# Moving the mapped product of attention one step earlier in a pipelined transformer block

## The chip, the cores and the metric

The kernel runs on one core of a Trainium2 chip. The metric is the device time of one execution in microseconds, the median of several. The core has TensorE (PE, matmuls), VectorE (DVE), ScalarE (ACT), GpSimd (POOL) and SyncE (SP, which here issues all DMAs). Each works through a program of its own; they meet only at semaphores. Matmul results land in PSUM, a memory of eight banks.

## The reference

One pre-normalised transformer block on x of 32 sequences, 256 tokens, 128 channels, in fp32:

```
x = x + attention(layernorm(x))        # 16 heads of 8, causal local window of 64
x = x + ffn(layernorm(x))

attention: q, k, v = x Wq', x Wk', x Wv'; query i sees key j with i-64 < j <= i
           softmax(q k' / sqrt(8)) v, then Wo
ffn:       scores = sigmoid(x gate_kernel) + bias, 16 experts in 4 groups
           the 2 best groups by the sum of their top 2, in them the 4 best experts
           weights normalised to sum 1, times 2.5
           y = sum over experts of weight * (silu(x w_gate) * (x w_up)) w_down
           + silu(x sw_gate) * (x sw_up) sw_down      # shared expert, width 128
```

## The kernel before

The work is cut into 16 groups (NG) of 2 sequences, 512 tokens each. One group passes through a chain of numbered stages (the constants `XT`, `QP`, `SC`, `PV`, `OT`, ... at the top), from 3 to 36. A slot has 8 steps (`STEPS`), and a stage n is done in step n % 8 of slot g + n // 8: five groups are under way at any time, so each step holds attention scores of one group, the expert work of an older one, and bits of others. Slots 0 to 3 and 16 to 19 are written out, slots 4 to 15 are a loop over pairs of slots. Each engine's block has a function `slot` that runs over the steps 0 to 7 and, within a step, over its pieces in a fixed order, written out by hand. That order and the semaphores are all that sets the time: an engine that waits holds everything behind it.

In each step there are, for one of eight units: gate and up projection on TensorE (L895 to L897, three matmuls each), tanh and a copy of the gate on ScalarE (`th` L597, `gate`), `tu` on VectorE (L798), two products on GpSimd (`gate2` L504, `hh` L509) and the down projection (L1077) one step later; and for one of eight attention units: a mask and scores on TensorE (L921, L933), row maxima on VectorE (`neg_max` L809), exponentials on ScalarE (`probs` L626), and a step later the transposition (`probsT` L765) and sums of the probabilities (`sums` L775).

Around the change, for each of the two halves b of a group (one sequence each):

- `turn_sums(b)` on VectorE (L783, L784): the reciprocals of the softmax sums, and their transposition. Stage `TURN[b]`.
- the spread on GpSimd (L482): each reciprocal is laid out by block of 32 queries, `by_block`. Stage `EXPAND[b]`. It waits for the transposition (`s_sum_t`).
- the spreading matmul on TensorE (L1037) with `to_channel`, which maps the reciprocals to channels, into a shared PSUM bank; then the mapped product on VectorE, `oT = o_f * bank` (L833), which is the last reader of that bank. Stage `OT + 4b`.
- the output projection (L1047) and the residual `H` (L840), stage `OW + 4b`; statistics for the second normalisation and, on GpSimd, the normalisation itself (L542 to L553, stages `LN2`, `LN2 + 4`), its transposition on TensorE (L1063, `XT2`), copied by ScalarE (`x_f`, `x_hi`).

Two PSUM banks are shared by many short uses (`RING`, `USES`): the attention inputs (`XT`, `QP`, `KP`, `VP`), the routing logits (`LG`, L963), the combine weights (`CT`, L1086), the shared expert (`SH`), `OT`, `OW`, `XT2`. The list is sorted by step and, within a step, by place (EARLY, POST, LATE, WEIGHTS), and the uses take the two banks in turn. TensorE, before it fills a bank (`free`), waits until the last use of that same bank has been taken by its reader. So the routing logits at the start of step 0 wait for whoever used their bank last, and so do the transposes of the combine weights in step 3, whatever data they need.

Of the kernel before, what the change touches and what calls it, by code (L numbers as in the profile page):

```python
# [49 lines left out]
SUMS = (11, 12, 13, 13, 14, 14, 15, 16)  # L50
TURN = (14, 16)
EXPAND = (15, 17)
OT, OW = 15, 16
LN2 = 17
# [16 lines left out]
    (EARLY, (VP, LG)), (LATE, (XT, QP, KP, XT2, XT2 + 4, SH)),  # L71
    (POST, (OT, OT + 4, OW, OW + 4, SH)), (WEIGHTS, (CT,)))
    for stage in stages])
# [11 lines left out]
def at(slot, s, stage, stride=1, count=1):  # L85

    for k in range(count):
        d = stage + k * stride
        if d % STEPS == s:
            off = d // STEPS  # L90
            if slot.fixed and not 0 <= slot.n - off < NG:
                return None, 0
            return Group(slot.n - off, (slot.par + off) % 2, slot.fixed), k
    return None, 0

# [87 lines left out]
def preln_block_kernel(nc, x, w_att, gate_b, w_gu, w_down, sw_down, consts, out):  # L183
    with ExitStack() as ctx:
# [269 lines left out]
        def _(pool):  # L454
# [8 lines left out]
            def slot(sl):  # L463
                for s in range(STEPS):
                    if sl.fixed and sl.n == 1 and s == PREPARE:
# [8 lines left out]
                           ALU.subtract).then_inc(s_cst, 1)  # L474
                    for b, stage in enumerate(EXPAND):
                        g, _ = at(sl, s, stage)
                        if g:
                            if not (g.fixed and g.n == 0):
                                taken(pool, slot_before(sl), (OT + 4 * b) % STEPS, POST)
                            pool.wait_ge(s_sum_t, g.n * GB + b + 1)  # L480
                            whole = [P, NQ, Q]
                            tt(by_block[:, b, :, :], sums_t[:, b, :].unsqueeze(1).broadcast_to(whole),  # L482
                               block_of[:, :].unsqueeze(2).broadcast_to(whole), ALU.mult).then_inc(s_exp, 1)
                    if sl.fixed and sl.n == 0 and s == LN1 + 1:
# [45 lines left out]
                    if g and part == 1:  # L530
# [4 lines left out]
                           sc3.rearrange("p n (g e) -> p n g e", e=4),  # L535
                           g_in[:, :, :].unsqueeze(3).broadcast_to([P, NT, N_GROUP, 4]), ALU.mult).then_inc(s_rp, 1)
                    g, b = at(sl, s, LN2, 4, GB)
                    if g:
# [130 lines left out]
        def _(dve):  # L669
# [72 lines left out]
            def slot(sl):  # L742
# [3 lines left out]
                for s in range(STEPS):  # L746
# [80 lines left out]

                    g, b = at(sl, s, OT, 4, GB)
                    if g:
# [32 lines left out]
                    if g and draining(sl):  # L862
                        dve.wait_ge(s_g2, g.n * NP + k + 1)
                        dve.wait_ge(s_tu, g.n * NP + k + 1)
                        v_.tensor_tensor(hh[:, k % 2, :], gate2[:, :], tu[:, k % 2, :], ALU.mult).then_inc(s_h, 1)  # L865
                    turn_sums(0)
                    sum_probs()
                    turn_sums(1)
                    g, _ = at(sl, s, YE)
# [20 lines left out]
        def _(pe):  # L890
# [48 lines left out]
            def slot(sl):  # L939
                for s in range(STEPS):  # L940
# [69 lines left out]
                    for turn_, stage in enumerate(PV):  # L1010
# [6 lines left out]
                        if not later and not (g.fixed and g.n == 0 and b == 0):  # L1017
                            taken(pe, slot_before(sl) if b else sl, (OT if b else OT + 4) % STEPS, POST)
                        pe.wait_ge(s_pt, g.n * NU + 4 * b + (4 if later else 3))
# [10 lines left out]

                    g, b = at(sl, s, OT, 4, GB)
                    if g:
# [7 lines left out]
                    if g:  # L1040
                        side, bank = free(POST)
                        taken(pe, sl if b else slot_before(sl), (OT + 4 * b) % STEPS, POST)
                        if g.fixed and g.n == 0 and b == 0:
                            pe.wait_ge(s_wf, 16 * FFN_LOADS)
                        for half in range(2):
                            r = slice(P * half, P * half + P)
                            ins = mm(bank[:, r], oT[:, r], wo[:, :], start=True, stop=True)  # L1047
                        ins.then_inc(s_filled[side], 1)
# [96 lines left out]
```

## Time and profile before

| | |
|---|---|
| median of 3 runs | 715.27 us (715.05 to 715.5) |
| profiled execution | 716.24 us, its span 714.4 us |
| TensorE busy | 659.0 us, 92% |
| VectorE busy | 588.1 us, 82% |
| ScalarE busy | 525.8 us, 74% |
| GpSimd busy | 495.6 us, 69% |
| mean granted clock of TensorE | 0.994 |

The span is the time between the first and the last instruction that the profile shows; the execution's own time has a little around it. Busy shares are sums of instructions' durations. A matmul's row ends after the next one has begun, so TensorE's rows overlap, and their sum isn't quite time in which nothing else could have run. In the timeline rows the bracket at the end gives the idle time of the engine ahead of the row, and who ended it.

### The profile page before, as it was taken

What the parts mean: (1) busy time and instruction counts of PE and PEld (TensorE: products, weight loads), DVE (VectorE), ACT (ScalarE), POOL (GpSimd) and SP (SyncE); (2) the same over time, 40 slices, a digit from 0 to 9 for tenths busy, and PEclk for the clock granted to TensorE, in tenths of its full rate; (3) what the DMA queues carried; (4) which work ended last, traced back from release to release, by engine and by line L of the source; (5) the groups of instructions that cost most, each with busy time, mean ns of one, the idle gap of its engine ahead of it and who ended that gap; (6) DMA issues with size and microseconds to landing.
All of it is one profiled execution on the core that took longest, in us unless ns stands there. A gap on an engine that the chain in (4) does not pass through costs nothing.

```text
span 714.4 us, 19501 instructions
## 1 busy us (share of the span) xinstructions
PE 659.0 (92%) x6232; PEld 521.2 (73%) x6232; DVE 588.1 (82%) x1710; ACT 525.8 (74%) x1603; POOL 495.6 (69%) x635
## 2 busy tenths in 40 slices
PE   3989889999999999999999999999999999989997
PEld 2877767777777777777777777777777777777875
DVE  3687888888889897889889897988979888897663
ACT  3786778697878878787887878787887878764332
POOL 4413367778778787878778777777878777876523
PEclk9999999999999999999999999999999999999999
DMA  5010032230403132140413123040322214040321
GB/s 173 1 32 30 2 101 66 59 123 11 141 29 119 59 105 73 40 138 2 142 34 119 59 76 102 2 147 29 119 59 96 82 32 119 15 135 33 118 77 45
DMA packets 50245, 52.60 MB, mean 74 GB/s; under 512 B 5664, under 2 KB 31904, under 8 KB 50080
## 3 DMA queue, kind: packets, MB, share of 16 engines
q1 hardware_dynamic: 50208, 52.14, 23.6%
q8 instruction: 20, 0.33, 0.2%
q14 instruction: 17, 0.14, 0.1%
HBM read 43.20 MB, written 4.72 MB: 67 GB/s over the span
## 4 chain that ended last, share of the span: by engine, by line
PE 42%; DVE 24%; ACT 19%; issue 10%; POOL 2%; DVEq 1%; DMA 1%; ACTq 0%; POOLq 0%; SPq 0%
ACT probs L626 9%; PE PS L1077 6%; PE PS L933 6%; DVE neg_max L809 6%; PE PS L895 5%; PE PS L1024 5%; PE PS L897 5%; PE PS L896 5%; ACT q_by_head L581 5%; DVE tu L798 4%; DVE probsT L765 3%; PE PS L1047 3%; DVE sums L775 3%; PE PS L963 2%; ACT k_by_row L581 2%
## 5 line engine op out<-in xcount | busy, mean ns | idle before, releaser
L626 ACT ACTIVATE probs<-PS,neg_max 128x96 f32<-128x96 f32 (+1 forms) x1024 | 246.8, 350 | 87.7 <-DVE neg_max L809 87.5
L504 POOL TENSOR_TENSOR gate<-gate,spread 128x512 f32<-128x512 f32 x124 | 158.1, 1275 | 96.6 <-ACT gate L581 40.8
L509 POOL TENSOR_TENSOR hh<-gate,tu 128x512 f32<-128x512 f32 x108 | 138.7, 1284 | 19.3 <-DVE tu L798 12.8
L809 DVE TENSOR_REDUCE neg_max<-PS 128x4 f32<-128x384 f32 (+1 forms) x256 | 121.6, 513 | 25.5 <-PE PS L933 25.0
L1077 PE MATMUL PS<-wd,hh 128*128 128x128 f32 x1024 | 137.9, 278 | 3.5 <-DVE hh L865 1.7
L1077 PEld LDWEIGHTS PS<-wd,hh 128*128 128x128 f32 x1024 | 126.5, 192 | 12.2 <-issue 4.3
L798 DVE SCALAR_TENSOR_TENSOR tu<-th,PS 128x512 f32<-128x512 f32 x128 | 87.4, 683 | 48.5 <-ACT th L597 36.6
L895 PE MATMUL PS<-x_hi,w_hi 128*128 128x512 f32 x288 | 125.0, 434 | 0.0
L897 PE MATMUL PS<-x_lo,w_hi 128*128 128x512 f32 x288 | 114.7, 398 | 0.0
L765 DVE STREAM_TRANSPOSE probsT<-probs 128x768 f32<-128x768 f32 (+1 forms) x128 | 114.4, 894 | 0.0
L896 PE MATMUL PS<-x_hi,w_lo 128*128 128x512 f32 x288 | 114.0, 396 | 0.0
L597 ACT ACTIVATE th<-PS 128x512 f32<-128x512 f32 x128 | 79.5, 621 | 42.6 <-PE PS L897 39.5
L933 PE MATMUL PS<-k_by_row,q_by_head 64*128 64x192 f32 (+2 forms) x1024 | 108.3, 318 | 0.0
L775 DVE TENSOR_REDUCE sums<-probs 128x8 f32<-128x768 f32 (+1 forms) x128 | 106.3, 851 | 0.0
L933 PEld LDWEIGHTS PS<-k_by_row,q_by_head 64*128 64x128 f32 x1024 | 84.6, 191 | 0.0
L581 ACT ACTIVATE gate<-PS 128x512 f32<-128x512 f32 x128 | 79.6, 622 | 0.0
L897 PEld LDWEIGHTS PS<-x_lo,w_hi 128*128 128x128 f32 x288 | 54.4, 189 | 12.7
L895 PEld LDWEIGHTS PS<-x_hi,w_hi 128*128 128x128 f32 x288 | 54.7, 190 | 10.8 <-issue 3.1
L896 PEld LDWEIGHTS PS<-x_hi,w_lo 128*128 128x128 f32 x288 | 54.7, 190 | 7.3
L921 PEld LDWEIGHTS PS<-band,ident 64*128 64x128 bf16 x320 | 14.4, 93 | 59.3 <-issue 30.2
L1024 PE MATMUL PS<-probsT,v_bd 128*32 128x96 f32 (+2 forms) x2048 | 51.1, 241 | 0.0
L921 PE MATMUL PS<-band,ident 64*128 64x256 bf16 (+2 forms) x320 | 38.8, 253 | 12.7 <-ACT probs L626 12.1
(107 smaller groups left out, 991.3 us busy)
## 6 DMA issues: line engine op xcount, KB each, us to landing
spread<-weights_by_expert SPq DMA_DIRECT2D x248, 128.0 KB, 3.0
X<-x SPq DMA_DIRECT2D x32, 256.0 KB, 3.6
OUT<-H SPq DMA_DIRECT2D x16, 256.0 KB, 3.0
out<-OUT SPq DMA_DIRECT2D x16, 256.0 KB, 3.8
ffn_stage<-w_gu SPq DMA_DIRECT2D x1, 1152.0 KB, 6.7
wd<-w_down SPq DMA_DIRECT2D x1, 512.0 KB, 6.8
weights_by_expert<-cT SPq DMA_DIRECT2D x16, 32.0 KB, 1.6
probsT<-w_att SPq DMA_DIRECT2D x1, 192.0 KB, 3.1
```

The source lines that it names most:

```text
L504: tt(gate2[:, :], gate[:, k % 2, :], spread[:, k % SP_BUFS, :], ALU.mult).then_inc(s_g2, 1)
L509: tt(hh[:, k % 2, :], gate2[:, :], tu[:, k % 2, :], ALU.mult).then_inc(s_h, 1)
L581: return nc.scalar.activation(dst, src, ACT.Copy, **kw)
L626: ins = nc.scalar.activation(probs[:, u % PROB_BUFS, tt, 2 * rows + e, j0:KW], PS[:, rows, n * KW + j0:n * KW + KW], ACT.Exp, bias=neg_max ...
L765: v_.transpose(probsT[:, b, :, t0:t0 + 2, c0:3, :].rearrange("p g t c q -> p t g (c q)"), probs[:, u % PROB_BUFS, :, :, c0 * Q:KW]).then_i ...
L775: v_.tensor_reduce(sums[:, b, HG * t0:HG * t0 + 2 * HG], probs[:, u % PROB_BUFS, :, :, j0:KW].rearrange("p t g k -> p (t g) k"), AX_X, ALU ...
L809: v_.tensor_reduce(neg_max[:, rows, :], src[:, :, j0:KW], AX_X, ALU.max, negate=True).then_inc(s_m, 1)
L895: mm(dst, l_hi, r_hi, start=True, stop=False)
L896: mm(dst, l_lo, r_hi, start=False, stop=False)
L897: return mm(dst, l_hi, r_lo, start=False, stop=True)
L933: ins = mm(dst[:, :, KW - nk:KW], q_by_head[r, g.par, q1 // Q - 1, :, :].rearrange("p v q -> p (v q)"), k_by_row[r, g.par, :, q1 - nk:q1], ...
L1077: ins = mm(PS[:, 7, r], hh[:, k % 2, r], wd[:, k, :], start=(k == 0 and n == 0), stop=(k == NP - 1), skip_group_check=True)
```

## The change

Nothing is computed in another way, and each engine has the same instructions. What differs is the steps:

- the reciprocals of the first half are turned at stage 13 instead of 14: in step 5, after the sums, instead of step 6, ahead of them (those of the second half stay at stage 16, step 0);
- the spread on GpSimd goes to the same stages as the turning (13 and 16), and its code stands after the routing pieces and ahead of the second normalisation, not at the start of a step;
- the spreading matmul and the mapped product go from stages 15 and 19 (steps 7 and 3) to 14 and 18 (steps 6 and 2). The shared banks are dealt out anew by the same rule.

```diff
-TURN = (14, 16)
-EXPAND = (15, 17)
-OT, OW = 15, 16
+TURN = (13, 16)
+EXPAND = (13, 16)
+OT, OW = (14, 18), 16
...
-    (POST, (OT, OT + 4, OW, OW + 4, SH)), (WEIGHTS, (CT,)))
+    (POST, (*OT, OW, OW + 4, SH)), (WEIGHTS, (CT,)))
...
+def either(slot, s, stages):
+
+    for b, stage in enumerate(stages):
+        g, _ = at(slot, s, stage)
+        if g:
+            return g, b
+    return None, 0
...
@@ GpSimd: gone from the start of a step, ahead of the products of the experts
-                    for b, stage in enumerate(EXPAND):
-                        g, _ = at(sl, s, stage)
-                        if g:
-                            if not (g.fixed and g.n == 0):
-                                taken(pool, slot_before(sl), (OT + 4 * b) % STEPS, POST)
-                            pool.wait_ge(s_sum_t, g.n * GB + b + 1)
...
@@ GpSimd: now behind the routing, ahead of LN2
+                    for b, stage in enumerate(EXPAND):
+                        g, _ = at(sl, s, stage)
+                        if g:
+                            if not (g.fixed and g.n == 0):
+                                taken(pool, slot_before(sl), OT[b] % STEPS, POST)
+                            pool.wait_ge(s_sum_t, g.n * GB + b + 1)
+                            whole = [P, NQ, Q]
+                            tt(by_block[:, b, :, :], sums_t[:, b, :].unsqueeze(1).broadcast_to(whole),
+                               block_of[:, :].unsqueeze(2).broadcast_to(whole), ALU.mult).then_inc(s_exp, 1)
                     g, b = at(sl, s, LN2, 4, GB)
...
@@ VectorE
-                    g, b = at(sl, s, OT, 4, GB)
+                    g, b = either(sl, s, OT)
...
-                    turn_sums(0)
                     sum_probs()
-                    turn_sums(1)
+                    for b in range(GB):
+                        turn_sums(b)
...
@@ TensorE
-                            taken(pe, slot_before(sl) if b else sl, (OT if b else OT + 4) % STEPS, POST)
+                            taken(pe, slot_before(sl) if b else sl, OT[1 - b] % STEPS, POST)
...
-                    g, b = at(sl, s, OT, 4, GB)
+                    g, b = either(sl, s, OT)
...
-                        taken(pe, sl if b else slot_before(sl), (OT + 4 * b) % STEPS, POST)
+                        taken(pe, sl if b else slot_before(sl), OT[b] % STEPS, POST)
```

On GpSimd, steps 5 to 7 of a slot of the loop before: the normalisation (`ve` to `xn`) follows the two products of step 5, and `by_block` stands behind step 6's.

```order
L504 TENSOR_TENSOR gate<-gate,spread 128x512
L509 TENSOR_TENSOR hh<-gate,tu 128x512
L542 TENSOR_TENSOR ve<-mv,eps 128x2
L547 TENSOR_TENSOR xn<-H,mv 128x256
L549 ISA
L550 TENSOR_TENSOR rs<-ve,half_neg 128x2
L552 REGISTER_ALU
L553 TENSOR_TENSOR xn<-xn,rs 128x256
L502 REGISTER_ALU
L504 TENSOR_TENSOR gate<-gate,spread 128x512
L509 TENSOR_TENSOR hh<-gate,tu 128x512
L362 REGISTER_ALU
L480 ISA
L482 TENSOR_TENSOR by_block<-sums_t,block_of 128x256
```

The same place now (all lines behind the change are 9 further on, L544 is the spread).

```order
L504 TENSOR_TENSOR gate<-gate,spread 128x512
L509 TENSOR_TENSOR hh<-gate,tu 128x512
L371 REGISTER_ALU
L542 ISA
L544 TENSOR_TENSOR by_block<-sums_t,block_of 128x256
L551 TENSOR_TENSOR ve<-mv,eps 128x2
L556 TENSOR_TENSOR xn<-H,mv 128x256
L558 ISA
L559 TENSOR_TENSOR rs<-ve,half_neg 128x2
L561 REGISTER_ALU
L562 TENSOR_TENSOR xn<-xn,rs 128x256
L502 REGISTER_ALU
```

`by_block` has passed the four instructions of the normalisation and the two products of step 6.

On TensorE, from the scores of step 6 to the logits of the next slot's step 0 before: L1037 is the spreading matmul, in step 7; the three matmuls from xT are the keys.

```order
L933 MATMUL PS<-k_by_row,q_by_head 128x192 x4
L947 REGISTER_ALU
L895 MATMUL PS<-xT_hi,w_hi 128x512
...
L1077 MATMUL PS<-wd,hh 128x128 x4
...
L933 MATMUL PS<-k_by_row,q_by_head 128x192 x4
L1036 ISA
L1037 MATMUL PS<-by_block,to_channel 128x256
L947 REGISTER_ALU
L1063 MATMUL PS<-cst,xn 128x128 x2
L1077 MATMUL PS<-wd,hh 128x128 x4
L963 MATMUL PS<-ffn_stage,x_f 128x16 x4
```

The same place now (L1046 is the spreading matmul, L972 the logits).

```order
L942 MATMUL PS<-k_by_row,q_by_head 128x192 x4
L956 REGISTER_ALU
L1045 ISA
L1046 MATMUL PS<-by_block,to_channel 128x256
L904 MATMUL PS<-xT_hi,w_hi 128x512
...
L1086 MATMUL PS<-wd,hh 128x128 x4
...
L942 MATMUL PS<-k_by_row,q_by_head 128x192 x4
L956 REGISTER_ALU
L1072 MATMUL PS<-cst,xn 128x128 x2
L1086 MATMUL PS<-wd,hh 128x128 x4
L972 MATMUL PS<-ffn_stage,x_f 128x16 x4
```

The spreading matmul stands ahead of the keys in step 6; step 7 goes from the scores to the transposes of the normalised rows.

## Rows read from the trace of the kernel before

**Rows 1.** Waits over the whole span: engine, line and whom for, us, times, longest us.

```profile
PE PS L963 <- DVE oT L833: 13.5, 14, 1.1
...
PE PS L1086 <- DVE oT L833: 5.7, 14, 0.7
```

**Rows 2.** Waits from 316 to 642 us, eight slots.

```profile
DVE neg_max L809 <- PE PS L933: 8.4, 9, 1.0
...
DVE H L840 <- PE PS L1047: 7.8, 16, 0.9
...
ACT cT L581 <- PE PS L1086: 2.9, 8, 0.4
```

**Rows 3.** TensorE in time, steps 6 to 0 (start, length, what, idle before).

```profile
309.36 0.50 PE L895 MATMUL PS<-xT_hi,w_hi 128*128 128x512 f32 x1
...
313.03 0.28 PE L921 MATMUL PS<-band,ident 64*128 64x256 bf16 x2 [0.41 <-ACT probs L626]
...
316.65 1.06 PE L963 MATMUL PS<-ffn_stage,x_f 128*128 128x16 f32 x8 [0.94 <-DVE oT L833]
```

**Rows 4.** VectorE in time, steps 5 to 7.

```profile
306.39 1.77 DVE L775 TENSOR_REDUCE sums<-probs 128x8 f32<-128x768 f32 x2
...
309.83 0.69 DVE L798 SCALAR_TENSOR_TENSOR tu<-th,PS 128x512 f32<-128x512 f32 x1 [1.04 <-ACT th L597]
...
312.26 0.31 DVE L783 RECIPROCAL sums<-sums 128x32 f32<-128x32 f32 x1
312.60 0.21 DVE L784 STREAM_TRANSPOSE sums_t<-sums 128x32 f32<-128x32 f32 x1
...
316.19 0.41 DVE L833 TENSOR_TENSOR oT<-o_f,PS 128x256 f32<-128x256 f32 x1
```

**Rows 5.** ScalarE in time, steps 5 and 7.

```profile
306.83 2.48 ACT L581 ACTIVATE q_by_head<-PS,queryrow 128x512 f32<-128x512 f32 x4
...
314.91 0.47 ACT L581 ACTIVATE x_f<-PS 128x256 f32<-128x256 f32 x1
```

**Rows 6.** GpSimd in time, steps 5 and 6.

```profile
307.67 0.19 POOL L542 TENSOR_TENSOR ve<-mv,eps 128x2 f32<-128x2 f32 x1
...
310.36 1.28 POOL L504 TENSOR_TENSOR gate<-gate,spread 128x512 f32<-128x512 f32 x1 [0.58 <-ACT gate L581]
311.72 1.29 POOL L509 TENSOR_TENSOR hh<-gate,tu 128x512 f32<-128x512 f32 x1
312.96 0.62 POOL L482 TENSOR_TENSOR by_block<-sums_t,block_of 128x256 f32<-128x256 f32 x1
```

**Rows 7.** TensorE in time, steps 3 and 4.

```profile
334.29 0.70 PE L1037 MATMUL PS<-by_block,to_channel 128*128 128x256 f32 x2
...
336.48 0.60 PE L1086 MATMUL PS<-cst,comb 128*16 128x128 f32 x4 [0.38 <-DVE oT L833]
336.84 0.48 PE L895 MATMUL PS<-x_hi,w_hi 128*128 128x512 f32 x1
...
338.74 0.26 PE L921 MATMUL PS<-band,ident 64*128 64x128 bf16 x4 [0.27 <-ACT probs L626]
```

**Rows 8.** VectorE in time, steps 2 and 4.

```profile
330.15 1.02 DVE L809 TENSOR_REDUCE neg_max<-PS 128x4 f32<-128x384 f32 x2 [1.04 <-PE PS L933]
...
341.00 0.42 DVE L840 TENSOR_TENSOR H<-PS,X 128x256 f32<-128x256 f32 x1 [0.46 <-PE PS L1047]
```

**Rows 9.** TensorE's routing logits in time, one opening each slot.

```profile
112.97 1.06 PE L963 MATMUL PS<-ffn_stage,x_f 128*128 128x16 f32 x8 [1.04 <-DVE oT L833]
438.87 1.06 PE L963 MATMUL PS<-ffn_stage,x_f 128*128 128x16 f32 x8 [1.05 <-DVE oT L833]
481.08 1.06 PE L963 MATMUL PS<-ffn_stage,x_f 128*128 128x16 f32 x8 [0.94 <-DVE oT L833]
603.20 1.06 PE L963 MATMUL PS<-ffn_stage,x_f 128*128 128x16 f32 x8 [0.94 <-DVE oT L833]
```

**Rows 10.** Windows of 4 us: length, five engines' busy time, clock, DMA.

```profile
438.00:442.00 4.00, 3.13 (x14) 2.48 (x14) 2.43 (x4) 4.00 (x13) 2.58 (x3) 0.76 0.32 97
```

More of the change, by code:

```diff
@@ L474, in slot @@
                            ALU.subtract).then_inc(s_cst, 1)
-                    for b, stage in enumerate(EXPAND):
-                        g, _ = at(sl, s, stage)
-                        if g:
-                            if not (g.fixed and g.n == 0):
-                                taken(pool, slot_before(sl), (OT + 4 * b) % STEPS, POST)
-                            pool.wait_ge(s_sum_t, g.n * GB + b + 1)
-                            whole = [P, NQ, Q]
-                            tt(by_block[:, b, :, :], sums_t[:, b, :].unsqueeze(1).broadcast_to(whole),
-                               block_of[:, :].unsqueeze(2).broadcast_to(whole), ALU.mult).then_inc(s_exp, 1)
                     if sl.fixed and sl.n == 0 and s == LN1 + 1:
```

## The prediction, made before the changed kernel ran

> **What bounds the kernel now.** I first read the busy shares. TensorE is busy 92% of the span and no other engine over 82%, yet that is no proof that it sets the pace: the chain of waits that ended last gives it 42%, VectorE 24%, ScalarE 19% and 10% to issue. So the end is set by a ring in which the three hand over to each other, and a microsecond counts only if all members of the ring get it. Next came the starts of the routing logits, the first work of each slot: they come at 112.97 and 603.20 us with eleven between them, so twelve slots of the loop take 490.2 us, 40.7 us each in eleven and 42.21 us in one (438.87 to 481.08) [rows 9]. What is worth something is what shortens those 40.7 us. The list of waits shows that TensorE stands in each slot for the same thing, the mapped product oT on VectorE: 13.5 us in 14 times before the routing logits and 5.7 us in 14 times before the transposes of the combine weights [rows 1]. That isn't data. Neither matmul reads oT; they want the shared bank that oT is the last reader of. Over eight slots the echo of this stands in four waits further on: VectorE's row maxima for the scores 8.4 us (about 1.04 per slot), H for the output projection 7.8 us in 16, cT on ScalarE 2.9 us in 8 [rows 2].
>
> I number the steps of a slot 0 to 7 as the code does, and take the slot that starts at 316.65 with the steps 5 to 7 before it.
>
> **Part 1: the wait ahead of step 0 goes.** The first half's mapped product leaves step 7 for step 6. The ring of banks is counted anew: 14 uses per slot as before, but in step 6 the product now stands between the values and the keys, so it takes the second bank, the keys take the first, and the logits of step 0 wait for the keys' copies, which end a step earlier. The logits then wait only for the copy x_f of step 7, which starts at 314.91 and takes 0.47 [rows 5]: they can start at 315.3 to 315.4 instead of 316.65 [rows 3], 1.25 to 1.35 us earlier (0.94 was idle, the rest is the spreading matmul that has left step 7). ScalarE's probabilities and copies in steps 7 and 0 run as before, since nothing there waits for TensorE, so the gain is banked only in step 2, where VectorE waits 1.04 us for scores before its maxima [rows 8]. This idle time is all that can be had there: VectorE is busy up to it. **Term: -1.04 us.**
>
> **Part 2: step 2 gets the second half's product.** It stands after the maxima and before the next transposition, so it costs its own 0.41 us [rows 4] on VectorE's part of the ring; the spreading matmul costs TensorE at most the 0.70 us of its row [rows 7], and TensorE has 1.3 us in hand by then. **Term: +0.41 us**, so the maxima of step 3 come 0.63 us earlier.
>
> **Part 3: step 3 loses it.** There VectorE ran tu, then oT, and only then could TensorE transpose the combine weights at 336.48 (0.38 us idle before) and go on to gate and up [rows 7]. Now the transposes need only the weights, which are there, and fit in the time in which TensorE would wait for tu; gate and up follow tu at once. That takes oT's 0.41 us out, and the transposes' own time, 0.36 us from their start to that of the gate's first matmul at 336.84 [rows 7]. **Term: -0.77 us.** ScalarE no longer waits 0.36 us for those transposes before cT [rows 2], which is the same gain seen on the other engine and isn't added. TensorE's 0.27 us before the mask of step 4 [rows 7] hangs on those probabilities and moves along. H in step 4 waits 0.46 us [rows 8], so VectorE takes up what it lags there.
>
> **Part 4: the reciprocals of the first half, turned at the end of step 5.** Reciprocal and transposition take 0.55 us (312.26 to 312.81 [rows 4]), the same instructions as before. In step 5 VectorE ends its sums at 308.16, transposes the values, and then idles 1.04 us until the tanh lets tu start at 309.83 [rows 4]. 0.55 of 1.04 is covered; ScalarE's run of four q_by_head copies from 306.83 to 309.31 [rows 5] is what hides it. Without that cover it would cost 0.55 us a slot. Step 6 loses 0.55 and gains oT's 0.41: nothing. **Term: 0**, bounds -0.14 to +0.55.
>
> **Part 5: the spread on GpSimd, ahead of the second normalisation.** For the second half nothing changes: the end of step 0 and the beginning of step 1 are one place on this engine. For the first half it moves from the start of step 7 to the middle of step 5 and brings a new wait: GpSimd now stands until VectorE has turned, 308.71, instead of starting the normalisation at 307.67 [rows 6]. Queued behind it are the normalisation (307.67 to 309.78, since 0.58 idle precedes 310.36), the weight times gate, and the hidden product. By their own durations: by_block 308.8 to 309.4, normalisation to 311.5, gate product to 312.8, hh to 314.15 instead of 313.01 [rows 6]. The hh of step 6 is wanted by the down projection of step 7, at about 314.1 when the spreading matmul has left that step. That is 0 to 0.15 us of waiting, hidden because the logits behind it wait for x_f until 315.3 anyway. The normalised rows are wanted at 313.9, so they have 2 us. **Term: 0**, bounds 0 to +1.1 (all of the delay, if that cover weren't there).
>
> **Part 6: the spreading matmul before the keys in step 6.** It needs by_block (309.4) and the bank that q_by_head leaves at 309.31, where the keys start today at 309.36 [rows 3, 5]. The keys go in behind it at about 310.0, with the values' bank free at 309.4. What follows is 0.6 us late, up to the mask of step 7 at 313.03, before which TensorE idles 0.41 us for ScalarE's probabilities [rows 3]; the other 0.2 us are covered since the tanh of step 7 is held by ScalarE's own key copies. **Term: 0**, bounds 0 to +0.6.
>
> **Sum.** Per slot -1.04 + 0.41 - 0.77 = -1.40 us. It holds in the 12 loop slots and in the one after them, 13 x 1.40 = 18.2. The fourteenth pair of waits is in slot 3, where half the work isn't there yet: I take 1.0 us. Later there is no attention left and TensorE simply works. 19.2 us in all, from the profiled execution's own 716.24 us (714.4 span and 1.84 around it) to 697.0; the median of the runs is 0.97 us below that execution, so **696.1 us**. No instruction is added or removed, so nothing else enters.
>
> The clock: in the one long slot the granted clock was 0.76 over 438 to 442 us [rows 10], so part of that stretch ran at 1.2 GHz and the rest at 2.4, and the slot took 1.5 us more than its neighbours [rows 9]; before its fall the engine had stood 1.05 us, as it did in other slots without a fall.
>
> The Trainium skill (TensorE: Matmul & The Clock Gate, HAM oscillation — how this bites in real kernels) says that idle gaps between bursts of matmuls bring the throttle back. By that rule, shorter gaps before the logits would make this fall go away, and the time would be 1.5 us lower, 694.6 us. The trace agrees only in part: gaps of that length are in every slot and the clock fell in one.
>
> **Rivals.**
> (a) Only part of it arrives. If something else on ScalarE or GpSimd holds step 3 so that part 3 gives nothing, the slot is left with -1.04 + 0.41 = -0.63 us: 13 x 0.63 + 0.5 = 8.7, 706.6 us. For it: the ring is tight, and ScalarE idles only in short pieces. Against it: ScalarE's waits in steps 3 and 4 are for this very chain [rows 2].
> (b) The clock's fall goes away as well: 694.6 us, as worked out above. Against: nothing singles that slot out.
> (c) Nothing is gained: the waits are replaced one for one. For this the logits would have to wait in the ring still, for the keys' copies; but these are ordered a whole step before. 715.
> (d) Slower, by one mechanism: the spreading matmul of step 6 waits on TensorE for by_block, with the keys, a down projection and gate and up of step 7 queued behind it. At by_block's end of 309.4 there is no wait. The slack behind is about 1.2 us (0.41 idle before the mask and what ScalarE's copies hide), and the gain eats 1.4 more: from an end at about 312.0 on, 2.6 us later than I put it, the kernel is slower. GpSimd would have to be held by the earlier hh or by the spread weights' DMA. At 3.1 us late a slot loses 0.5: 13 x 0.5 = 6.5, 721.8 us. Against: GpSimd is free at 307.67 [rows 6].
>
> **Chances.** Forecast 0.55 (with its own range 692 to 701), (b) 0.10, (a) 0.22, (c) 0.05, (d) 0.08. The range for all takes the low end from (b) with part 1 giving 1.25 instead of 1.04 and slot 3 giving 2: 691; the high end is (a), 707, and it leaves out (c), (d) and a little below. What this kernel's measurement can tell from no change is 0.2%, 1.4 us. Faster 0.87, same 0.05, slower 0.08.
>
> **What would show it.** In the changed kernel: no wait of the logits or of the combine transposes for oT; slots of about 39.3 us between logits; by_block of the first half ending about 1.2 us after the sums of step 5, with GpSimd waiting some 1.0 us there; the maxima of step 2 without their 1.04 us; tu in step 6 still waiting for the tanh, not for the turn. I am wrong if the loop's slots stay above 40.1 us, if TensorE waits for by_block in step 6 by more than 0.3 us, or if the down projection of step 7 waits for hh by more than 0.5 us.

## The result, and the profile after

The changed kernel takes 692.38 us (median of 4 runs, 691.17 to 692.62) against 715.38 us for the kernel before (the median of the 4 runs taken with it; the 715.27 us above is that of the first 3): a ratio of 0.9673, 95% interval 0.9656 to 0.9689. That is 23.0 us, where 19.2 us had been worked out. The profiled execution took 692.62 us with a span of 690.8 us; instructions are the same in number, and TensorE is busy 95% of the span (657.7 us, against 659.0 before).

Whom the routing logits (now L972) wait for, over the whole span: reason, us, times. This answers to [rows 1].

```profile
its engine sat idle before it (us, times) until:
  issue: 0.5, 1
  ACT x_f L590: 0.2, 1
```

The 13.5 us for oT are gone, and no row for the combine transposes (now L1095) waiting for oT is left either. The waits from 316 to 642 us, answering to [rows 2]:

```profile
POOL by_block L544 <- DVE sums_t L793: 11.1, 9, 2.2
...
DVE H L849 <- PE PS L1056: 2.1, 3, 0.9
PE PS L1046 <- POOL by_block L544: 2.1, 8, 0.6
...
ACT cT L590 <- PE PS L1095: 0.7, 1, 0.7
```

VectorE's maxima no longer wait for TensorE at all in this list (8.4 us before), H waits 2.1 instead of 7.8 us, cT 0.7 instead of 2.9. Two waits are new: GpSimd for the turned sums, and a little of TensorE for by_block (0.16 to 0.24 us in the loop, 0.62 us once behind it, at 612.96). The first logits of the first and last loop slot and of the next one, answering to [rows 9]:

```profile
111.63 1.06 PE L972 MATMUL PS<-ffn_stage,x_f 128*128 128x16 f32 x8
...
580.30 1.04 PE L972 MATMUL PS<-ffn_stage,x_f 128*128 128x16 f32 x8
...
618.58 0.96 PE L972 MATMUL PS<-ffn_stage,x_f 128*128 128x16 f32 x8
```

Twelve loop slots take 468.67 us, 39.06 each, against 490.23. Two neighbouring slots without a fall of the clock (307.32 to 385.32) take 78.00 us, 39.00 each, against 40.73 (316.65 to 398.10). So the 23.6 us between the two spans are: 1.37 in slot 3 (35.46 against 36.83 us), 21.56 in the loop, of which 1.5 are the clock's fall at 440 us that this execution doesn't have there, 0.36 each in slots 16 and 17, and nothing before and after.

Not all loop slots gain the same. Slots 6 to 15 gain 1.7 us each, but slots 4 and 5 (from 111.63 and 151.00 us) still take 39.37 and 39.48 us, at full clock. There GpSimd's product of gate and weights in step 5 stands 1.34 and 1.86 us for the DMA of the spread weights, and TensorE 0.31 and 0.82 us for the hidden product behind it; from slot 6 on the DMA costs GpSimd about 0.5 us and TensorE nothing.

One slot on each engine. TensorE (start, length, what, idle before), answering to [rows 3, 7]:

```profile
307.32 1.04 PE L972 MATMUL PS<-ffn_stage,x_f 128*128 128x16 f32 x8
...
326.61 0.60 PE L1095 MATMUL PS<-cst,comb 128*16 128x128 f32 x4
327.21 0.50 PE L904 MATMUL PS<-x_hi,w_hi 128*128 128x512 f32 x1
...
340.40 0.70 PE L1046 MATMUL PS<-by_block,to_channel 128*128 128x256 f32 x2 [0.23 <-POOL by_block L544]
340.75 0.59 PE L904 MATMUL PS<-xT_hi,w_hi 128*128 128x512 f32 x1
```

The logits at 307.32 follow without a wait for a bank; the transposes at 326.61 have none either, and the gate's matmul at 327.21 comes right when tu of step 3 (326.48, 0.68 long) is done. The keys (340.75) stand behind the spreading matmul, which waited 0.23 us for by_block. VectorE, answering to [rows 4, 8]:

```profile
320.87 1.02 DVE L818 TENSOR_REDUCE neg_max<-PS 128x4 f32<-128x384 f32 x2
...
323.00 0.41 DVE L842 TENSOR_TENSOR oT<-o_f,PS 128x256 f32<-128x256 f32 x1
...
325.57 1.00 DVE L818 TENSOR_REDUCE neg_max<-PS 128x4 f32<-128x384 f32 x2
...
331.13 0.42 DVE L849 TENSOR_TENSOR H<-PS,X 128x256 f32<-128x256 f32 x1
...
337.19 1.77 DVE L784 TENSOR_REDUCE sums<-probs 128x8 f32<-128x768 f32 x2
338.99 0.35 DVE L792 RECIPROCAL sums<-sums 128x32 f32<-128x32 f32 x1
339.38 0.21 DVE L793 STREAM_TRANSPOSE sums_t<-sums 128x32 f32<-128x32 f32 x1
...
340.62 0.69 DVE L807 SCALAR_TENSOR_TENSOR tu<-th,PS 128x512 f32<-128x512 f32 x1 [0.34 <-ACT th L606]
```

The maxima of step 2 (320.87) have no idle time before them, H (331.13) none, the turning (338.99, 339.38) lies behind the sums of step 5, and tu of step 6 still waits for the tanh. GpSimd, answering to [rows 6]:

```profile
300.67 0.61 POOL L544 TENSOR_TENSOR by_block<-sums_t,block_of 128x256 f32<-128x256 f32 x1 [1.18 <-DVE sums_t L793]
...
303.31 1.29 POOL L504 TENSOR_TENSOR gate<-gate,spread 128x512 f32<-128x512 f32 x1
304.68 1.28 POOL L509 TENSOR_TENSOR hh<-gate,tu 128x512 f32<-128x512 f32 x1
...
339.74 0.61 POOL L544 TENSOR_TENSOR by_block<-sums_t,block_of 128x256 f32<-128x256 f32 x1 [1.24 <-DVE sums_t L793]
```

It stands 1.18 and 1.24 us for the turned sums; the hidden product of step 6 ends at 305.96, and the down projection that wants it starts at 306.10 without a wait.

### The profile page after: what moved, and what is told of

Its sections match the earlier page's. It is cut to its first block, busy times and chain, and to the rows that moved or that the text cites. A ratio compares the mean times of both kernels' runs of the same rounds, so it can differ in the third digit from the quotient of the medians.

```text
span 690.8 us, 19501 instructions
## 1 busy us (share of the span) xinstructions
PE 657.7 (95%) x6232; PEld 519.9 (75%) x6232; DVE 587.3 (85%) x1710; ACT 522.6 (76%) x1603; POOL 496.1 (72%) x635
## 4 chain that ended last, share of the span: by engine, by line
PE 45%; DVE 21%; ACT 11%; issue 11%; POOL 9%; DMA 1%; DVEq 1%; POOLq 0%; ACTq 0%; SPq 0%
PE PS L1086 8%; PE PS L904 6%; ACT probs L635 6%; PE PS L942 5%; PE PS L906 5%; PE PS L905 5%; DVE neg_max L818 4%; PE PS L1033 3%; DVE sums L784 3%; DVE probsT L774 3%; POOL hh L509 3%; POOL gate L504 2%; PE PS L1056 2%; PE PS L1046 2%; PE PS L930 2%
## 5 line engine op out<-in xcount | busy, mean ns | idle before, releaser
L544 POOL TENSOR_TENSOR by_block<-sums_t,block_of 128x256 f32<-128x256 f32 x32 | 19.7, 616 | 49.7 <-DVE sums_t L793 49.7
```

## The experiments

Slot times below are from two neighbouring undisturbed loop slots, logits to logits, in the profile of each run: 40.73 us in the kernel before, 39.00 in the changed one. The two neighbours aren't quite equal: in the changed kernel the even slots, the ones behind the loop's jump back, take 39.09 us and the odd ones 38.91. Times are medians, with the ratio to the kernel before, run beside them on the same chip (714.6 to 715.1 us).

**1. Is it the bank or the place of the product?** (e1) Nothing moves; XT2 comes ahead of OT in the list of uses, and its `taken`, `filled` and `free` follow.

```diff
-    (EARLY, (VP, LG)), (LATE, (XT, QP, KP, XT2, XT2 + 4, SH)),
+    (EARLY, (VP, LG, XT2, XT2 + 4)), (LATE, (XT, QP, KP, SH)),
```

> The kernel before with every piece of work in its old step; only the two banks are dealt otherwise: the transposes of the normalised rows (XT2) now come ahead of the spreading matmul in the list of uses, so in steps 7 and 3 the two swap banks. The logits of step 0 and the combine transposes of step 3 then wait for ScalarE's copy x_hi instead of for oT. Theory (the wait was for the bank, not for the product): x_hi is done about 0.9 us before oT in step 7 and 0.5 us before it in step 3, so most of the gain comes without moving anything: 696 to 702 us. Rival 1 (what counts is where VectorE does the product and the turning): no more than a third of the gain, 708 to 715 us.

697.26 us, ratio 0.9761 (0.9739 to 0.9782); slot 39.49 us. 1.24 of the 1.73 us come with every instruction in its old step. The waits of this run from 270 to 610 us:

```profile
DVE neg_max L809 <- PE PS L933: 3.2, 9, 0.4
...
DVE H L840 <- PE PS L1047: 1.9, 9, 0.5
```

There is no wait for oT in its list. VectorE still waits 0.3 to 0.4 us per slot before the maxima of step 2. TensorE in step 7 shows the most of it:

```profile
306.18 0.69 PE L1037 MATMUL PS<-by_block,to_channel 128*128 128x256 f32 x2 [0.29 <-ACT k_by_row L581]
...
307.84 1.07 PE L963 MATMUL PS<-ffn_stage,x_f 128*128 128x16 f32 x8
```

The spreading matmul is still in step 7, and now stands 0.29 us for a bank that ScalarE's key copies hold; the transposes and the down projection follow it without idle time up to the logits. The copy x_hi (307.41, 0.38 us long) ends at 307.79, just ahead of the logits at 307.84, so whether the logits' own wait for their bank costs anything here isn't shown. The theory holds: most of the loss was a bank held by a reader in which the waiting matmul had no interest.

**2 and 3. The two halves apart.** (e2, e3)

```diff
 e2: turning and spread as before
+TURN, EXPAND = (14, 16), (15, 17)
+OT, OW = (15, 18), 16
 e3: turning and spread as in the changed kernel
+OT, OW = (14, 19), 16
```

> Only the second half's product moves, from step 3 to step 2 (OT 15, 18; turning and spread as in the kernel before). By my terms the slot gets +0.41 - 0.77 = -0.36 us, 13 times: 4.7 us, 710 to 711 us, and the logits keep their wait for oT of 0.94 to 1.05 us. Rival (the two parts only work together, since TensorE lacks the 1.3 us of slack that part 1 gives): the spreading matmul in step 2 delays the maxima of step 3 by its own 0.54 us and the time is 714 to 718 us.

> Only the first half moves (OT 14, 19; turning and spread as in the changed kernel); the combine transposes of step 3 still wait for oT. By my terms -1.04 us per slot, 13 times, and 0.6 in slot 3: 14.1 us, 701 to 702 us. Rival (the terms don't add; the first alone lifts the bound, and the second is only what was left): 694 to 697 us. Second rival (the gain of the first part is lost again in step 3, where oT and the copy of cT stand in a row): 706 to 710 us.

e2: 708.85 us, ratio 0.9927 (0.9900 to 0.9955), slot 40.13: 0.60 us gained where 0.36 was expected, and the time 1.2 us under the 710 to 711 that I had given. e3: 701.0 us, ratio 0.9800 (0.978 to 0.982), slot 39.60: 1.13 gained where 1.04 was expected. 0.60 + 1.13 = 1.73, the whole of the change: the parts add, and neither needs the other. e3 keeps the other wait; its TensorE in step 3 and 4 looks as in [rows 7]:

```profile
291.99 0.61 PE L1095 MATMUL PS<-cst,comb 128*16 128x128 f32 x4 [0.37 <-DVE oT L842]
...
294.26 0.26 PE L930 MATMUL PS<-band,ident 64*128 64x128 bf16 x4 [0.26 <-ACT probs L635]
```

e2's time is less good than its slot, since three of its loop slots took 41.6 us. One of its windows of 4 us (length, busy times, granted clock, DMA) shows why:

```profile
352.00:356.00 4.00, 4.00 (x26) 3.10 (x26) 2.08 (x3) 3.18 (x9) 2.27 (x3) 0.69 0.32 115
```

**4. The spread's place on GpSimd.** (e4) Its block stands behind LN2.

```diff
-                    for b, stage in enumerate(EXPAND):   # ahead of LN2
...
+                    for b, stage in enumerate(EXPAND):   # behind LN2, ahead of first_norm
```

> The changed kernel with one thing undone: on GpSimd the spread stands behind the second normalisation, not ahead of it. The first half's by_block then ends about 1.0 us later relative to the sums of step 5, the normalisation 0.6 to 1.0 us earlier. Theory (TensorE in step 6 stands for by_block, the keys queue behind, but there is 0.4 us of idle time before the mask of step 7 and some cover behind): 0 to 0.4 us per slot slower than the changed kernel, 692.4 to 697.5 us. Rival (the normalisation is what matters, by_block has time): 0 to 0.3 us per slot faster, 688.5 to 692 us.

701.33 us, ratio 0.9819 (0.9800 to 0.9839); slot 39.44, 0.44 us more than the changed kernel (0.50 over the ten slots 6 to 15, 39.48 against 38.98). TensorE in step 6:

```profile
343.26 0.70 PE L1046 MATMUL PS<-by_block,to_channel 128*128 128x256 f32 x2 [1.08 <-POOL by_block L562]
```

1.08 us for by_block instead of 0.23: 0.85 us more, of which 0.44 reach the slot. The slot's cost is a little above the upper end that I gave (0.4), and the time 3.8 us above it; outside those ten slots, slots 3 and 4 are longer too, 36.45 and 40.61 us instead of 35.46 and 39.37. The rival, by which by_block has time, is out. The cover behind the spreading matmul is thus about 0.4 us beyond what it already waits, not the 1.2 us with which rival (d) was priced.

**5 and 6. The keys ahead of the spreading matmul.** (e6: alone; e7: with the spread behind)

```diff
 TensorE's block of a step:
-                    g, b = either(sl, s, OT)   # ahead of OW, QP, KP
...
+                    g, b = either(sl, s, OT)   # behind KP, ahead of XT2
```

> The changed kernel with the keys ahead of the spreading matmul on TensorE in step 6, so that they don't queue behind its wait for by_block (0.17 to 0.23 us in the trace). Theory (that wait is nearly covered by what ScalarE does): 0 to 0.1 us per slot faster, 691 to 692.5 us. Rival (the queue behind the wait is on the path of the slot): 0.2 us per slot faster and more, 688.5 to 690 us.

> The keys ahead of the spreading matmul on TensorE, and the spread behind the second normalisation on GpSimd. Putting the spread behind cost 0.46 us per slot, with TensorE standing 1.1 to 1.3 us for by_block in step 6. Theory (the loss came through what was queued behind that matmul, the keys above all): with the keys ahead most of it is gone, but a down projection and gate and up of step 7 still queue, so 0.1 to 0.3 us per slot above the changed kernel, 693 to 697 us. Rival (the loss came because the mapped product itself is late on VectorE): no better than with the spread behind alone, 698 to 702 us.

e6: 694.71 us, ratio 0.9712 (0.9693 to 0.9732), slot 39.00, unchanged. e7: 699.76 us, ratio 0.9770 (0.9742 to 0.9798), and its slot is 39.00 as well. TensorE in e7, step 6, keys and then the spreading matmul (here L1065):

```profile
346.26 0.50 PE L904 MATMUL PS<-xT_hi,w_hi 128*128 128x512 f32 x1 [0.17 <-DVE v_keys L800]
...
347.14 0.70 PE L1065 MATMUL PS<-by_block,to_channel 128*128 128x256 f32 x2
```

In slots 6 to 15 e4's loss is gone whole, not only in most part: it came through the keys queued behind the wait, and the late product cost VectorE nothing. In slots 4 and 5 it isn't gone. There the DMA of the spread weights holds GpSimd 1.57 and 1.87 us, the spread comes later still, TensorE waits 0.43 and 0.45 us for by_block, and VectorE stands for the product, which is the rival's mechanism:

```profile
192.27 0.42 DVE L842 TENSOR_TENSOR oT<-o_f,PS 128x256 f32<-128x256 f32 x1 [1.13 <-PE PS L1065]
```

As a time, 699.76 us lies outside the theory's 693 to 697 and inside the rival's 698 to 702, so it is the slots that decide here. The 8.2 us between the profiled executions of e7 (700.84) and the changed kernel (692.62) are: 2.65 before the first logits (78.82 instead of 76.17), 1.99 in slot 3, 1.26 in slots 4 and 5 (40.01 and 40.1 instead of 39.37 and 39.48), and 2.24 in slot 16 (40.52 instead of 38.28). Windows of 4 us near 50, 64, 82 and 622 us show granted clocks of 0.61, 0.60, 0.59 and 0.64, so falls lie in all of these stretches but slots 4 and 5, where the clock is full. The changed kernel has one fall ahead of its first logits too, at 44 to 52 us.

e6's 694.71 us is slower than either of its expectations, and why isn't shown: its profiled execution took 692.75 us with a slot of 39.00, as good as the changed kernel's 692.62, and its other three runs, of which there is no trace, took 694.49 to 695.34 at granted clocks of 0.991 to 0.995.

**7. Was the turning hidden?** (e5) A second reciprocal and transposition behind the first half's turning.

```diff
+                            if b == 0:
+                                v_.reciprocal(extra[:, 0, :], sums[:, b, :])
+                                v_.transpose(extra[:, 1, :], sums[:, b, :])
```

> The changed kernel, with a second reciprocal and a second transposition (into a tile that nobody reads) behind the turning of the first half in step 5: 0.55 us more on VectorE, and nothing that the spread waits for is later. In the changed kernel's trace VectorE idles 0.34 to 0.36 us before tu of step 6. Theory (the turning was hidden under ScalarE's q_by_head copies, and 0.35 us of the cover are left): 0.2 us per slot, 2.5 us in 12 to 13 slots, 694 to 696 us. Rival (VectorE's end of step 5 is on the path, so the turning wasn't free): the full 0.55 us per slot, 7 us, 699 to 700 us. Second rival (tu of step 6 has cover behind it too): 692 to 693 us.

693.46 us, ratio 0.9688 (0.9658 to 0.9718), slot 39.00. VectorE in it:

```profile
339.51 0.21 DVE L794 STREAM_TRANSPOSE sums_t<-sums 128x32 f32<-128x32 f32 x1
339.64 0.31 DVE L796 RECIPROCAL extra<-sums 128x32 f32<-128x32 f32 x1
339.87 0.15 DVE L797 STREAM_TRANSPOSE extra<-sums 128x32 f32<-128x32 f32 x1
339.95 0.67 DVE L804 STREAM_TRANSPOSE v_keys<-PS 128x512 f32<-128x512 f32 x1
340.75 0.69 DVE L811 SCALAR_TENSOR_TENSOR tu<-th,PS 128x512 f32<-128x512 f32 x1
```

This execution runs 0.12 us behind the changed kernel's (logits at 307.44 and 307.32), and the values' transposition starts at 339.95 instead of 339.57. So the extra pair moved it by only 0.26 us, not by the 0.55 us that I had put; nothing waits between its two instructions. The cover left was 0.34, so some 0.1 us of it remains, and tu stands where it stood, relative to the logits. The 0.2 us per slot of the theory didn't come, but neither was the cover overrun, so this run doesn't tell the theory from the second rival, by which tu has cover behind it as well. It does rule out the first rival: the turning is free.

**8. What sets the slot now?** Four kernels. e8 moves the first normalisation's statistics (1.2 us of VectorE) from step 3 to the end of step 7 of the slot before; e11 the same, ahead of the probabilities' transposition in step 7; e9 and e10 leave out one of the three matmuls of the up projection, in the changed kernel and in the one before; e12 is e11 and e9 together.

```diff
 e8, e11 (x is loaded a slot earlier; the loop ends at slot 13)
+                    if s == STEPS - 1 and not (sl.fixed and not 0 < sl.n < NG - 1):
+                        g = Group(sl.n + 1, 1 - sl.par, sl.fixed)
...
+                        stats(sl, X[:, g.par, :, :], NT, st1, mv1).then_inc(s_mv1, 1)
 e9, e10, e12
-                exact3(PS[:, 5, :], *w2(WU + P * k), *x2).then_inc(s_u, 1)
+                mm(PS[:, 5, :], u_hi, x2[0], start=True, stop=False)
+                mm(PS[:, 5, :], u_lo, x2[0], start=False, stop=True).then_inc(s_u, 1)
```

> The changed kernel with one more piece moved: the statistics of the first normalisation (four bn_stats, four bn_aggr, 1.2 us on VectorE) go from step 3 to the end of step 7 of the slot before, where VectorE idles 1.66 us for the tanh; x is loaded a slot earlier for it, and the loop covers two slots fewer. Theory (VectorE sets the pace from the maxima of step 2 to tu of step 5, and has time to spare at the end of step 7): the slot loses up to 1.2 us until TensorE, 95% busy, binds: 0.5 to 0.9 us per slot, 680 to 686 us. Rival (TensorE already sets the pace in steps 2 to 5): nothing, 691 to 693 us. Second rival (the statistics end too late in step 0 and push tu): slower, 693 to 700 us.

> The changed kernel without the third matmul of each up projection (high part of the weights times low part of the input), so its result is less exact: 8 matmuls of 0.23 us less per slot on TensorE, 1.85 us, and nothing else. Theory (in the changed kernel TensorE itself sets the slot: its rows fill 38.67 of 38.91 us): the slot shortens by 1.3 to 1.85 us, and with the slots of the drain the time falls by 20 to 30 us, to 662 to 673 us. Rival (the ring of waits still sets it, and TensorE being full is a coincidence): less than 0.6 us per slot, above 682 us.

> The kernel before with the same eight matmuls per slot left out. Theory (its slots were set by the waits for oT, TensorE had 2.1 us of idle time per slot): where TensorE is on the ring, in steps 0 to 2, the gain is real until VectorE's 1.04 us before the maxima of step 2 are used up, and in steps 3 and 4 it stays for oT; 0.7 to 1.2 us per slot, less than the changed kernel gains, and with the drain 14 to 21 us: 694 to 701 us. Rival (TensorE's work sets both kernels alike): the same gain as in the changed kernel, 20 to 30 us, 685 to 695 us.

| | time, us | ratio, 95% interval | undisturbed slot, us |
|---|---|---|---|
| e8 | 707.31 | 0.9904 (0.9869 to 0.9940) | 38.91, every second one 43.0 |
| e9 | 688.04 | 0.9608 (0.9570 to 0.9647) | 38.78 |
| e10 | 709.34 | 0.9921 (0.9896 to 0.9945) | 40.02 |
| e11 | 697.27 | 0.9754 (0.9738 to 0.9771) | 38.94, every second one 40.3 |
| e12 | 689.83 | 0.9660 (0.9629 to 0.9692) | 38.54, every second one 39.7 |

The windows of one slot (length, then TensorE's busy time first) gave the theory for e9, in the kernel before and in the changed one:

```profile
316.65:357.43 40.78, 38.59 (x379) 30.51 (x380) 35.48 (x106) 32.74 (x102) 32.25 (x41) 1.00 0.26 78
```

```profile
307.32:346.23 38.91, 38.67 (x380) 30.50 (x380) 35.27 (x106) 32.27 (x101) 32.09 (x41) 1.00 0.25 81
```

TensorE's rows fill 38.6 to 38.7 us in both; before, 2.2 us of a slot were left over, now 0.24. I took this for the sign that TensorE sets the slot. The theory fell: with 1.85 us of matmuls less, the slot lost 0.22 us, and the time of 688.04 us is the rival's (above 682), not the 662 to 673 of the theory. The rows overlap, and part of what fills them is time in which the next matmul would not have come earlier. e10 lost 0.71 us per slot, at the lower end of what was expected, but more than e9 and not less, as had been expected too; and its time, 709.34 us, is outside both expectations (694 to 701, 685 to 695), since three of its loop slots took 41.6, 41.5 and 43.1 us, with granted clocks of 0.64, 0.57 and 0.50 in windows of 4 us there. That leaving TensorE work out helps the kernel before more may come from some of it having lain between two waits; this isn't shown.

e8's odd slots take 38.91 us, as the changed kernel's odd slots do: they gained nothing, so VectorE's 1.2 us in step 3 weren't the limit either. Its every second slot is lengthened by 4 us, and the time of 707.31 us is outside all three expectations. VectorE there, at the loop's jump back, and TensorE behind it:

```profile
354.95 0.28 DVE L704 BATCH_NORM_AGGREGATE mv<-st 128x2 f32<-128x6 f32 x3
358.87 0.69 DVE L807 SCALAR_TENSOR_TENSOR tu<-th,PS 128x512 f32<-128x512 f32 x1 [3.65 <-issue]
359.62 0.79 PE L910 MATMUL PS<-x_hi,w_hi 128*128 128x512 f32 x1 [2.54 <-DVE tu L807]
```

TensorE stands for it 2.2 to 2.5 us in each of the four jumps, and in each its clock then falls (0.63 to 0.68 in the next window of 4 us), so part of the 4 us is the price of a fall. Something else is new in this kernel. This is the DMA queue that brings instructions (packets, MB, share), over the whole span, in the changed kernel and in e8:

```profile
q14 instruction: 17, 0.14, 0.1%
```

```profile
q14 instruction: 42, 0.34, 0.2%
```

e11 and e12 have 43 and 42 packets, every other kernel here 17 or 18. Between 200 and 500 us, with the loop running, the kernel before and the changed one load no code at all; e8, e11 and e12 load 17 packets of 8 KB there, and in e8 one of them falls into the 3.65 us in which VectorE stands.

> As the run with the statistics of the first normalisation moved into step 7 of the slot before, but ahead of the transposition of the probabilities and not at the step's end. There every second slot (the one behind the loop's jump back) took 43.0 us, with VectorE idle 3.65 us before tu of step 0 and no releaser, and the others 38.9 to 39.0 us. Theory (VectorE's program can only jump back once the last wait inside the statistics is over; ahead of the sums there is time for it): no slot of 43 us, slots 38.8 to 39.0 us since TensorE's rows fill 38.7, and 688 to 692 us. Rival (the long slots come from the loop having changed its length or from loading x a slot earlier): the 43 us slots stay, 704 us and more.

> The same, and without the third matmul of each up projection (result less exact, 1.85 us per slot less on TensorE). Taking only the matmuls out of the changed kernel gave 0.23 us per slot (39.0 to 38.77), taking only the statistics out of step 3 gave nothing in the undisturbed slots. Theory (two limits lie within 0.2 us of each other: TensorE's work of 38.7 us, and a ring of VectorE in steps 1 to 5 and ScalarE in steps 6 to 0 of 38.77 us without any TensorE in it): only both together move the slot, to 37.3 to 38.1 us, 668 to 680 us. Rival (a third thing, GpSimd or the chain from cT through memory to the spread weights, holds the slot): no more than 0.3 us below 38.77, above 681 us.

With the statistics ahead of the last transposition and sums, the long slots are 1.3 to 1.4 us above their neighbours instead of 4.1. Not all of this is the place of the last wait before the jump: TensorE's clock fell in each of e8's long slots and in none of e11's, and elsewhere a fall costs 1.4 to 1.6 us. VectorE stands 1.5 to 1.7 us there without a releaser, instead of 3.45 to 3.65. The time of 697.27 us is outside both expectations. The loading of code is in e11 as it is in e8, so the rival, that the long slots come from the loop having changed, isn't out: it may be that with the moved statistics the loop's code has to be loaded again in each round, and that the last wait only decides how late the load starts. The queue's rows don't name the engine, so this is argued, not shown. e12 was to show two limits close together, one of TensorE and one of VectorE and ScalarE, with 37.3 to 38.1 us when both are relieved. It gave 38.54, 0.37 below the changed kernel's odd slots, and 689.83 us, as the rival has it (above 681): this theory fell as well. VectorE in e12, step 4:

```profile
328.51 0.69 DVE L807 SCALAR_TENSOR_TENSOR tu<-th,PS 128x512 f32<-128x512 f32 x1 [0.40 <-ACT th L606]
...
330.33 0.42 DVE L849 TENSOR_TENSOR H<-PS,X 128x256 f32<-128x256 f32 x1 [0.47 <-PE PS L1064]
```

Of the 1.2 us taken out of step 3, 0.87 come back as waits in step 4, for the tanh and for the output projection. Which chain holds the slot at 39 us is left open. It isn't TensorE's work alone, nor VectorE's in step 3, nor both: taking out the matmuls gives 0.22 us, the statistics nothing, both 0.37. None of the variants beats the changed kernel with all of the computation in it.

## Why the prediction was right

The time (692.38) lies in the range (691 to 707) and in the likeliest case's own (692 to 701), near its low end; 19.2 us were worked out and 23.0 came. Step by step:

- **The ring, and the bank as its weak point**: right. e1 takes 1.24 us per slot from the bank alone, with every instruction in its old place.
- **Part 1, -1.04 us**: measured -1.13 (e3). On VectorE, from tu of step 7 to the maxima of step 2, 15.50 us became 14.42 in the changed kernel, -1.08.
- **Parts 2 and 3, +0.41 and -0.77**: measured together -0.60 (e2) instead of -0.36. From the maxima of step 2 to those of step 3 it is +0.34 (4.37 to 4.71 us in e2); from there to tu of step 4 -0.53 (4.67 to 4.14), and from that to tu of step 5 -0.40 (5.07 to 4.67). The third term was mis-sized: I counted the time that leaves TensorE's queue in step 3, 0.77 us, and dismissed H's wait of 0.46 us in step 4 as something in which VectorE only takes up what it lags. It was 0.40 us to be had, for the output projection comes earlier by as much as everything else on TensorE; 0.93 us in all.
- **Part 4, 0**: right, with the cover that was named (e5).
- **Part 5, 0**: right. GpSimd waits 1.2 us (1.0 said), the hidden product of step 6 is late by as much as worked out, and the down projection doesn't wait.
- **Part 6, 0**: right here, with 0.16 to 0.24 us of waiting in the loop (under 0.3 said), and by less than I thought. I gave the queue behind the spreading matmul 1.2 us of slack; e4 shows some 0.4. Rival (d) would have begun to bite much sooner, though from 0.44 us per slot to a slower kernel is still a long way. e7 shows for slots 6 to 15 that its mechanism, the keys queued behind the wait, is the real one.
- **The sum**: right in its result, with single terms off. The loop gave 12 x 1.67 = 20.1 us (the fall of the clock left out; 1.7 in slots 6 to 15, 1.44 and 1.29 in slots 4 and 5) where 12 x 1.40 = 16.8 were put, slot 3 1.37 where 1.0 was put, slot 16 only 0.36 where 1.40 was put. In slot 16 GpSimd waits 3.83 us for the spread weights (4.64 before), and TensorE 1.00 us for what GpSimd makes of them; most of what TensorE had gained ran into that. The low value of slot 16 makes up for part of the third term's error, which is luck.
- **Rival (b), the clock**: the loop's fall at 440 us isn't in the changed kernel's profile, but others are, at 44 to 52 us and at 688 us. The forecast leaves the clock as it was, so the 1.5 us of this fall are in the 23.0 and not in the 19.2. e7, with the same slots from 6 to 15, has more falls; e2, with gaps of 0.94 to 1.05 us in each slot, has three; e4, in which TensorE stands 1.01 to 1.33 us for by_block in each slot, has none in its loop; e8 has one after each of its four gaps of 2.2 to 2.5 us. The rule of the Trainium skill (TensorE: Matmul & The Clock Gate, HAM oscillation — how this bites in real kernels) that gaps bring the throttle back fits e8, and e2 against the changed kernel's loop; it doesn't fit e4's loop, and doesn't tell e7 from the changed kernel.

## What to carry to other kernels

A wait for a buffer is told from a wait for data by asking what the waiting instruction reads; where it reads nothing of the releaser's, dealing the buffers out in another order may bring most of the gain with nothing moved. When an instruction is moved to an earlier step on an in-order engine, price not its own wait but what queues behind it, and give every idle time downstream in the same ring its part of the gain before calling it absorbed. An engine whose rows fill the slot is not thereby the one that sets it: take some of its work away and look. And when a variant of a loop gets slower for no reason that its waits show, look whether it loads code while it runs.

## What the runs showed of the hardware

- TensorE's clock falls in some slots and costs 1.4 to 1.6 us a time (41.6 against 40.1 us in e2, 42.2 against 40.7 in the kernel before, 41.5 and 41.6 against 40.0 in e10). TensorE had stood 1.05 us just before the falls of the kernel before and of e2, but it stood 1.01 to 1.33 us in each loop slot of e4 without a fall, and after 2.2 to 2.5 us in e8 it fell each of four times.
- Kernels with the same slot differ in time: 692.4 us for the changed kernel, 699.8 for e7, both with 39.00 us per slot. Of the 8.2 us between their profiled executions, 6.9 lie in stretches with falls of the clock and 1.3 in two slots without one. In e7's runs the time goes with the mean granted clock, 697.53 us at 0.995 and 700.84 at 0.988, but the clock isn't all: e1's runs go from 696.41 us at 0.999 to 698.86 at 1.0. Differences of 1 or 2 us between variants here are best read from the slots.
- At the loop's jump back VectorE can stand for 3.65 us with no releaser (e8), and 1.5 to 1.7 us when its last wait comes earlier (e11). Both kernels load code within the loop, 17 packets from 200 to 500 us, where the changed kernel loads none; that the one causes the other isn't shown.
